# A four-layer transformer block on one core: the self attention takes the keys first and scores in the same pair's steps, and the cross attention moves its reciprocal product, its rounding and its sums to other steps

## The reference

```python
x = x + tanh(g_xattn[0]) * L0_xattn(layernorm(x), ctx_2048, ...)   # a scan over the context
x = x + tanh(g_ffn[0]) * L0_ffn(layernorm(x), ...)                 # 8 experts
x = x + tanh(g_xattn[1]) * L1_xattn(layernorm(x), ctx_2048, ...)   # self and cross attention
x = x + tanh(g_ffn[1]) * L1_ffn(layernorm(x), ...)                 # shared and routed experts
```

```python
q  = _ln(fp8_linear(ln_out, wq,  ...))     # 16 heads
k  = _ln(fp8_linear(ln_out, wk,  ...));  v = fp8_linear(ln_out, wv, ...)   # 8 groups
core = gqa(q, k, v)                        # self attention over 56 positions
qx = _ln(fp8_linear(ln_out, wqx, ...))
kx, vx = split(cond @ w_kv_x.T);  kx = _ln(kx)
xout = gqa(qx, kx, vx)                     # cross attention over 1500 positions
catq = div_clamp_fp8(concat([core, xout]), proj_smooth)
return catq @ wproj.T * (proj_in_scale * proj_w_scale)
```

## Time and profile before

| | us |
|---|---|
| median of 3 runs | 2896.24 (2894.05 to 2896.83) |
| the profiled execution, its own time | 2896.9 |
| its span, first to last instruction | 2895.1 |
| PE busy | 2545.1 (88%) |
| DVE busy | 2156.1 (74%) |
| ACT busy, POOL busy | 1100.6, 928.2 |

### The profile page before, as it was taken

One profiled execution on the slowest core, in us unless ns is written; L12 is line 12 of the kernel. 1 busy time (PEld: TensorE's weight loads), 2 busy tenths in 40 slices (PEclk: granted clock), 3 DMA queues, 4 the chain that ended last, 5 costly groups with the idle time before them and its releaser, 6 DMA issues. The chain is left out here.

```text
span 2895.1 us, 39559 instructions
## 1 busy us (share of the span) xinstructions
PE 2545.1 (88%) x13434; PEld 2221.3 (77%) x13434; DVE 2156.1 (74%) x3892; ACT 1100.6 (38%) x1787; POOL 928.2 (32%) x584
## 2 busy tenths in 40 slices
PE   7999999939999957777699999999999999986797
PEld 5777777738999945666588888888888888875797
DVE  8777777773333367777488889999999999993377
ACT  1000000014444445556144444545444444444332
POOL 6560000000000012443255555555555555553000
PEclk9999999969999958888799999999999999998899
DMA  6444333120111030101322122222222222213311
GB/s 240 182 172 158 137 143 135 55 73 30 59 44 44 0 115 26 39 39 39 118 73 70 62 73 73 73 73 71 70 66 68 69 69 65 65 38 86 103 50 40
DMA packets 116412, 231.89 MB, mean 80 GB/s; under 512 B 22176, under 2 KB 94704, under 8 KB 112240
## 3 DMA queue, kind: packets, MB, share of 16 engines
q1 hardware_dynamic: 112880, 218.35, 22.2%
q0 software_dynamic: 3456, 12.58, 1.1%
HBM read 158.95 MB, written 71.96 MB: 80 GB/s over the span
## 5 line engine op out<-in xcount | busy, mean ns | idle before, releaser
L1358 POOL TENSOR_TENSOR s_acc<-s_acc,s_sx 125x896 f32<-125x896 f32 x128 | 356.4, 2784 | 249.0 <-ACT s_sx L1422 248.9
L290 DVE BATCH_NORM_STATS2 s_st<-ps 125x6 f32<-125x128 f32 x1536 | 316.2, 286 | 114.2 <-PE ps L246 112.4
L1422 ACT ACTIVATE s_sx<-s_sx 125x896 f32<-125x896 f32 x192 | 184.0, 959 | 461.4 <-DVE s_sx L1574 461.3
L1505 PE MATMUL ps<-s_p_hi,s_cn_hi 125*128 125x448 f32 x768 | 297.7, 388 | 7.3 <-DVE s_p_lo L1580 6.9
L1468 PE MATMUL ps<-s_qc_hi,s_ct_hi 128*125 128x448 f32 x768 | 294.5, 383 | 1.3 <-issue 1.3
L1556 DVE TENSOR_TENSOR s_sx<-ps,keep_krs 125x896 f32<-125x896 f32 x192 | 208.7, 1087 | 106.8 <-PE ps L1468 103.2
L1468 PE MATMUL ps<-s_qc_lo,s_ct_hi 128*125 128x448 f32 x768 | 286.0, 372 | 0.0
L1468 PE MATMUL ps<-s_qc_hi,s_ct_lo 128*125 128x448 f32 x768 | 285.4, 372 | 0.0
L1505 PE MATMUL ps<-s_p_lo,s_cn_hi 125*128 125x448 f32 x768 | 283.1, 369 | 0.0
L1505 PE MATMUL ps<-s_p_hi,s_cn_lo 125*128 125x448 f32 x768 | 282.8, 368 | 0.0
L246 PE MATMUL ps<-s_wk_hi,s_hi 128*125 128x512 f32 x768 | 246.5, 402 | 40.3 <-DVE s_st L290 21.8
(11 more groups left out here) (303 smaller groups left out, 6054.9 us busy)
## 6 DMA issues: line engine op xcount, KB each, us to landing
s_raw<-in_ctxt SPq DMA_DIRECT2D x16, 1500.0 KB, 7.3
ct_hi<-s_hi SPq DMA_DIRECT2D x16, 1500.0 KB, 10.4
ct_lo<-s_lo SPq DMA_DIRECT2D x16, 1500.0 KB, 13.6
s_ct_hi<-ct_hi SPq DMA_DIRECT2D x48, 500.0 KB, 3.8
s_ct_lo<-ct_lo SPq DMA_DIRECT2D x48, 500.0 KB, 4.5
s_cn_raw<-in_ctx SPq DMA_DIRECT2D x48, 500.0 KB
s_w<-in_w SPq DMA_DIRECT2D x16, 1024.0 KB, 5.3
qx<-s_qxs SPq DMA_DIRECT2D x16, 448.0 KB, 2.8
```

The source lines that it names most:

```text
L290: ins = dve.bn_stats(st[:, G * t + g, :], kx[0:TT, t % NB, g // 4, DH * (g % 4):DH * (g % 4) + DH])
L1358: pool.tensor_tensor(a, a, p[:, PR * w.pt:PR * w.pt + PR, :], ALU.add).then_inc(s["acc_ready"], 1)
L1422: act.activation(p, p, ACT.Exp).then_inc(s["exp_ready"], 1)
L1505: mm = pe.matmul(pv[:, k, :], x[:, t, k * P:k * P + P], y[w.vr][:, j, :], start=(t == 0 and c == 0), stop=(t == NT - 1 and c == 2))
```

## The change

The order of the chunks becomes keys, queries, cross queries, values (`TURN_OF`, `ORDER`), so that a pair's queries and keys are ready after six chunks. Scores and maxima move into slots 7 to 11 of the pair's own turn; exponentials, sums, products and outputs into slots 0 to 7 of the next (the last output into slot 0 of the turn after that). Values are the last input, and their quantisation moves from before the first turn, and from slot 0, to slot 4 of a couple's first turn. In the cross attention DVE's `ca` moves from step 0 into step 5 of the unit before, `cb`, `ce`, `cc` and POOL's `cs`, `cat` from step 0 to step 3, PE's sums from step 2 to step 3 behind the scores; DVE's second `qc_lo` goes ahead of step 3's scaling, and PE's wait for it moves from step 4 to the sums in step 3. No arithmetic is added or taken away.

```diff
-KIND = [0] * NQ + [1] * NQ + [2] * NK + [3] * NK
+PART = [0] * NQ + [1] * NQ + [2] * NK + [3] * NK
+TURN_OF = [2, 0, 1, 3]
+ORDER = [c for part in TURN_OF for c in range(CHUNKS) if PART[c] == part]
+KIND = [TURN_OF.index(PART[c]) for c in ORDER]
...
-        SCORES, MAXIMA, EXPS = (0, 1, 2, 3), (1, 2, 3, 4), (5, 5, 5, 5)
-        SUMS, TURNED, VALUES, OUTPUT = (6, 7, 7, 8), (8, 9, 10, 11), (9, 10, 11, CHUNKS), (10, 11, CHUNKS, CHUNKS + 5)
-        SCALED, QUANTISED = ({}, {7: 0, 9: 1, 10: 2, 11: 3}), ({0: 3}, {8: 0, 10: 1, 11: 2})
+        SCORES, MAXIMA, EXPS = (7, 8, 9, 10), (8, 9, 10, 11), (CHUNKS,) * 4
+        SUMS, TURNED = [tuple(CHUNKS + t for t in ts) for ts in ((1, 2, 2, 3), (3, 4, 5, 6))]
+        VALUES, OUTPUT = [tuple(CHUNKS + t for t in ts) for ts in ((4, 5, 6, 7), (5, 6, 7, CHUNKS))]
+        SCALED, QUANTISED = ({3: 3}, {3: 0, 9: 1, 10: 2}), ({4: 3}, {4: 0, 10: 1, 11: 2})
...
-                for kind in range(4):
+                for kind in range(3):
                     round_input(0, kind)
...
                 def scores(q, a):
-                    if a == 0:
-                        pe.wait_ge(s["tr_read"], NORMED * q + NORMED)
+                    pe.wait_ge(s["tr_read"], NORMED * q + NK + a + 1)
...
-                        if early(p, 1) and t == 8:
+                        if early(p, 1) and t == 4:
                             pe.wait_ge(s["wk_loaded"], 16)
...
-                    if w.i == 0 and w.three_back:
+                    if w.i == 3 and w.three_back:
                         d = w.u - 3
                         pool.wait_ge(s["cc_ready"], d + 1)
...
+                    if w.i == 3 and w.two_back:
+                        pe.wait_ge(s["acc_ready"], NPR * (w.u - 1))
+                        if w.one_back:
+                            pe.wait_ge(s["mt_read"], w.u)
+                        if w.new and w.next:
+                            pe.wait_ge(s["qc_lo_ready"], K2 * w.u + 2 * K2)
+                        for j in range(HG):
+                            mm = pe.matmul(sums[:, j:j + 1], acc[w.h][:, 0, PAIR * j:PAIR * j + PAIR], keep.ones[0:TT, 0:1], start=True, stop=True)
...
+                    if w.i == 3 and w.next and w.new:
+                        qc_split(w.u + 1, 1 - w.h, 1)
...
+                    if w.i == NPR - 1 and w.two_back:
+                        dve.wait_ge(s["rb_read"], w.u - 1)
+                        dve.wait_ge(s["v_ready"], w.u - 1)
+                        dve.tensor_tensor(ca[:, :], misc[:, 0:QH], rsc[:, :], ALU.mult).then_inc(s["v_read"], 1)
```

More of the change, by code:

```diff
@@ L194, in _ @@
                 for c in range(CHUNKS):
-                    j, kind = c % 2, KIND[c]
+                    j, kind = c % 2, PART[c]
                     if c >= 2:
@@ L714 @@
 NORMED = CHUNKS - NK
-LAST = [NQ - 1, 2 * NQ - 1, 2 * NQ + NK - 1, CHUNKS - 1]
-KIND = [0] * NQ + [1] * NQ + [2] * NK + [3] * NK
+PART = [0] * NQ + [1] * NQ + [2] * NK + [3] * NK
+TURN_OF = [2, 0, 1, 3]
+ORDER = [c for part in TURN_OF for c in range(CHUNKS) if PART[c] == part]
+KIND = [TURN_OF.index(PART[c]) for c in ORDER]
+LAST = [max(c for c in range(CHUNKS) if KIND[c] == kind) for kind in range(4)]
 RING = 3
@@ L785, in self_attention @@
         beyond = lambda p: isinstance(p, int) and p >= NP
-        slots = lambda p: range(max(OUTPUT) + 1 if beyond(p) else CHUNKS)
+        slots = lambda p: range(max(OUTPUT) - CHUNKS + 1 if beyond(p) else CHUNKS)
         def at_slot(table, t, p, act):
             for a in range(NQ):
[L791 to L794, removed]
+                back, left = divmod(table[a] - t, CHUNKS)
+                if left == 0 and back >= 0 and not early(p, back) and not beyond(p - back if isinstance(p, int) else p):
+                    act(p - back, a)
         def input_work(table, t, i, r, act):
-            if t in table[r] and not (isinstance(i, int) and (i >= COUPLES or i == 0 and r == 0 or i == COUPLES - 1 and r == 1)):
+            if t in table[r] and not (isinstance(i, int) and i + r >= COUPLES):
                 act(i + r, table[r][t])
@@ L966, in turn @@
                             weight_hi(t + AHEAD)
-                        if early(p, 1) and t == 9:
+                        if early(p, 1) and t == 5:
                             act.wait_ge(s["wk_psum"], 1)
@@ L977, in turn @@
                         input_work(SCALED, t, i, par, scale_input)
-                        if live and t == EXPS[0]:
+                        if live and t == EXPS[0] - CHUNKS:
                             std_of(p, t + 1)
@@ L1193, in _ @@
                     weight_lo(c)
-                for kind in range(1, 4):
+                for kind in range(1, 3):
                     quantise(0, kind)
@@ L1521, in run @@
                         pe.wait_ge(s["qc_lo_ready"], K2 * w.u + K2 + 1)
-                    if w.i == 2 and w.two_back:
-                        pe.wait_ge(s["acc_ready"], NPR * (w.u - 1))
-                        if w.one_back:
-                            pe.wait_ge(s["mt_read"], w.u)
-                        for j in range(HG):
-                            mm = pe.matmul(sums[:, j:j + 1], acc[w.h][:, 0, PAIR * j:PAIR * j + PAIR], keep.ones[0:TT, 0:1], start=True, stop=True)
-                        mm.then_inc(s["sum_ready"], 1)
                     if w.i == 2 and w.new and w.next:
@@ L1585, in run @@
                         dve.tensor_reduce(m4[:, :], misc[0:PAIR, 0:HG * TT].rearrange("p (g n) -> p g n", g=HG), AX.X, ALU.max).then_inc(s["mt_read"], 1)
+                    if w.i == 3 and w.three_back:
+                        dve.wait_ge(s["v_read"], w.u - 2)
+                        if not (static(b) and w.u < 4):
+                            dve.wait_ge(s["cat_ready"], w.u - 3)
+                        dve.tensor_scalar(cb[:, :], ca[:, :], FP8_MAX, -FP8_MAX, ALU.min, ALU.max).then_inc(s["cb_ready"], 1)
+                        dve.wait_ge(s["cb_ready"], w.u - 2)
+                        dve.tensor_scalar(ce[:, :].bitcast(U16), cb[:, :].bitcast(U16), 0x7F80, None, ALU.bitwise_and).then_inc(s["ce_ready"], 1)
+                        dve.wait_ge(s["ce_ready"], w.u - 2)
+                        dve.tensor_scalar(cc[:, :], ce[:, :], 2.0 ** -6, 1.5 * 2.0 ** 20, ALU.max, ALU.mult).then_inc(s["cc_ready"], 1)
                     if w.new and w.i >= 1:
```

50 lines of the change are left out of this document (18 added, 32 removed).

## The result

The changed kernel takes 3088.6 us (median of 4 runs, 3085.5 to 3092.1) where the kernel before takes 2895.8 (the median of 4 by now): a ratio of 1.0667, interval 1.0648 to 1.0685. The prediction was 2851, range 2817 to 2884. It is slower by 193 us, and no rival had that: the slowest, (d), stood at 2899.

A forecast was written before the change was run, and what follows sets the result against it. The prediction took the ring of ACT and DVE to bound the self attention and PE the cross attention. Its terms, -12.2 - 2 - 8.8 - 40 + 8 + 10 + 3 - 3 = -45, gave about 2851 us, range 2817 to 2884.

The forecast's parts named there:

- (d): Cross attention, units with h = 1: `mx` behind `cn_lo`, PE waits 4 us or more, clock falls; about 2899, chance 0.08.
- The clock, -3: PE in the cross attention: falls to 1.2 GHz after idle time should go; -3 us, bounds -6.5 and +27.
- The end, -12.2: End of the self attention: PE turns the first probabilities about 7.9 us after the last normalisation instead of 20.1; -12.2 us.
- The start, -2: Start of the self attention: the fourth input's quantisation leaves it; -2 us.
- The turns, -8.8: Self attention's turns: even 37.3 to 35.4 us, odd 41.3 to 38.5, pair 0 loses 4; -8.8 us in all.
- nothing given back: Self attention's turns: the bound of -20 us, with no moved work costing time in other slots.
- The sums, -40 and +8: Cross attention: PE's sums find `acc` ready behind step 3's scores, -40 us; they now wait for the second `qc_lo`, +8.
- `ca` and `mx`, +10 and +3: Cross attention: `ca` ahead of step 5's maximum puts `mx` behind `cn_lo`; transposes wait longer, +10 us, next unit's first product, +3.
- (b): Cross attention gives all: PE idles nowhere and `mx` slips in ahead; 2802 us, chance 0.12.
- (a): Cross attention gives nothing: new waits of 4 us a batch replace those removed; 2873 us, chance 0.17.

The follow-up runs named there:

- e2: The changed kernel with the loads of context chunks 2 and 0 each put ahead of the store they stood behind in SP's queue: 2906.3 us.
- e5: The changed kernel with both stores in SP's queue behind every load ready earlier, the next body's `cn` and `q` included: 2824.9 us (0.9745).
- e4: The kernel before with the self attention's part of the change alone: 2862.5 us (0.9884).
- e10: e5 with POOL waiting for the unit's `mx` before the last `cn_lo` of a batch: 2800.5 us (0.9675).
- e6: The changed kernel with `cb`, `ce`, `cc`, `cs` and `cat` back in step 0, SP's order untouched: 2894.5 us (0.9988).
- e7: e6 with `ca` back in step 0 too: 2871.6 us (0.9905).
- e8: e5 with `ca` behind both maxima of step 5 instead of ahead of them: 2849.0 us (0.9832).
- e9: The kernel before with e5's order of SP's queue and nothing else: 2896.2 us (0.9996).
- e12: e5 with the second `qc_lo` behind step 3's scaling again, PE's wait for it still ahead of the sums: 2900.1 us (1.0016).

## Why the prediction was wrong, point by point

- **The step that failed** is in the part on the cross attention: it priced the move of `cb`, `ce`, `cc`, `cs` and `cat` to step 3 by DVE's and POOL's holds alone ("`cs` and `cat` now also stand in steps 3 and 4"), and followed it no further than POOL. The next to wait for `cat` is SP's store, and behind that stand the loads of the context. The trace of before would have told it. Its timeline of SP's queue, and PE's first scores with that chunk:

```profile
1931.40 0.37 SPq L1317 DMA_DIRECT2D cat<-s_cat  x1
1932.02 0.57 SPq L1299 DMA_DIRECT2D s_ct_hi<-ct_hi  x1
1932.68 0.56 SPq L1300 DMA_DIRECT2D s_ct_lo<-ct_lo  x1
1933.79 7.16 SPq L1305 DMA_DIRECT2D s_cn_raw<-in_ctx  x3
1941.22 4.11 SPq L1311 DMA_DIRECT2D s_q<-qx  x1
...
1943.13 0.37 PE L1468 MATMUL ps<-s_qc_hi,s_ct_hi 128*125 128x448 f32 x1
```

  A store, and 0.6 us behind it a load, then more: loads that are issued right after a store were waiting for it. PE uses the chunk from step 4's scores on, at 1943.13. Three steps are 18.8 us (three twelfths of 75.1), so the load of `ct_lo`, issued at 1932.68, would be issued at 1951.5 and land 4.5 later (the page's median) at 1956.0: an estimate of 12.9 us late by these rows alone, and 12.35 was measured. The same working finds the wait for `q`: issued at 1941.22, it would be issued at 1960.0 and land 11.8 later (its median) at 1971.8, where PE wants it at 1965.82; e2's row has 4.07 us. For chunk 0 it gives only 0.5 us (1969.23 + 18.8 + 4.5 against PE's scores at 1991.97), where 3.78 was measured. The rest would be the place of `cat` behind POOL's `acc` and `cn_lo`; no run separates it. The term that was missing from the sum is 16.1 us of wait and 3.9 of clock a batch, less the 1.6 before the transposes that the wait swallows: 18.4 by the two windows, 264 us in all (3088.6 - 2824.9). It was missing, not mis-sized.
- **The clock, -3**: right in sign without the waits for loads. In e5 PE is busy for 1147.9 us over the cross attention where it was 1157.0, so -9, and the batch above is at 1.00. In the changed kernel the batch is at 0.91.
- **The end, -12.2**: from the last L1138, 1336.8, to the last `cats` are 27.4 us where there were 38.2, -10.8. **The start, -2**: the first L1138 is at 1056.5, 2.6 earlier. Both held.
- **The turns, -8.8**: mis-sized. They gave 19.6 (the first L1138 of pair 7 is 22.2 earlier, 2.6 of it the start), which is the bound of "nothing given back". An odd turn takes 36.8 and not 38.5, an even one 34.4 to 35.0 and not 35.4, and pair 0 lost nothing where +4 was forecast: its turn takes 38.5 for 38.8. What PE does for `wk` in slot 4 stretched one slot from 3.75 to 4.55. A quantisation was put at 1.3; it stretches its slot by 0.7 (3.34, and 2.60 in pair 7, which has none). The three last slots take 7.2 and 8.9 where 6.7 and 10 were forecast. The recorded sum was also off in itself: its own terms give -2.2 and -3.0 a turn and not -1.9 and -2.8, 1.3 us in all. The whole self attention gives 33, by e4, in place of 23.
- **The sums, -40 and +8**: L1486 stands 13.8 us in e5, 26.2 less than L1528 before; forecast was 32 less. The wait for `qc_lo` comes in 27 units, not in 16, at 0.57 and 0.2 in turn.
- **`ca` and `mx`, +10 and +3**: the prediction's mechanism held: `mx` stands behind `cn_lo` in the units with h = 1, and e10 shows it by taking it away. That `ca`'s place brings this is shown by e6 against e7; that the moved rounding alone would bring it too (e8) was not seen. L1524 stands 26.2 us in e5, released by `mx`, where L1514 had 24.8, released by `ca`: +1.4 in place of +10. No wait of the first product has grown. `ce` is at 278 ns, as forecast, and `cb` at most at 393, so the rounding nowhere stands behind an `acc` in step 3. What this pays was undervalued: the rounding back in step 0 costs 70 us (e6 against e5, if SP's order is worth nothing there, as e9 has it for the kernel before), and with it there the move of `ca` alone costs 23 (e6 against e7).
- The Trainium skill (SBUF — State Buffer, section "Who interferes with whom") says that DVE's and POOL's shared ports go to whoever issues first, for its whole instruction. By that, POOL's wait for `mx` should free it, and the trace of e10 agrees: 0.62 us where e5 has 2.67 behind `cn_lo`.
- **Altogether**: with the missing term taken out (e5), the prediction's sum, 2851, stands against 2824.9. 10 of the 26 us between them are the self attention's. The other 16 are the cross attention's, which gave 37.6 (e5 against e4) for 22. Of those 16, the idle time before the transposes and the first product makes about 12 (+1.4 for +13), the clock 6, PE's wait for `p_lo` 3, which the prediction had not looked at; the sums take 6 back. Rival (b), "the cross attention gives all", named 2802, and e10 measured 2800.5; but e10 has a wait that the change has not, and 10 us more from the self attention than (b) had. The waits of 4 us on DVE of rivals (a) and (d) did not come (2.7 at most in e5).

What stays open: whether the wait for `qc_lo`, the last in e10 that an order of instructions could take, can be taken away. The trace of e5 says what holds it up. Where PE waits 0.57 (1925.86), DVE's maximum L1605 ends just ahead of it, at 1925.27, and DVE is late by a `p_lo` of 2.21 us beside POOL's `cn_lo`. Where PE waits 0.19 (1963.40), `qc_lo` itself waits 0.56 for ACT's `qc_hi` (L1386). No other order was tried.

## What to carry to other kernels

When a step is moved, follow its result past the engines to the queues: name each DMA that waits for it, and each DMA behind that one, however little it has to do with it. A store in a load queue is a gate, and the diff does not show it, since not one line of that queue changes. In the trace it shows as a load issued within a microsecond of a store, again and again. Shift the pair by the moved steps, add the load's time to landing, and compare with the first instruction that wants the data: here that gives the wait of 12.35 us to within one. And an idle time of two microseconds on PE, repeated in each unit, costs more than its length: in e12 2.8 us of it a batch brought 2.4 of busy time through the clock, in e8 0.5 us of it brought 1.4.

## What was not expected of the hardware

- The load of `q` (448 KB) took 12.7 us to land in e2, where three loads of `cn` (500 KB each) had been issued just ahead of it, and 3.3 in e5, where the last of them had been issued some 9 us ahead. SP's row for issuing it reads 4.07 us in e2 and 0.36 in e5.
- PE's clock fell behind some of the waits of 1.9 us that came in every unit (e12, 0.96 and 0.98) and behind those of 2.03 to 2.09 in every second unit (e8, at 1808, 1883 and 1958 us, 0.98), and not where they were of 0.6 and, in every second unit, of 1.6 (e5, 1.00).
